# Reordering the head of an eight-core attention and feed-forward kernel: statistics tile by tile, GpSimd's rows as add then multiply, and one key unit of pair 1 in each token group

## The reference, cut to what matters

```
x = x + attn_block(layernorm(x))           # per batch entry x is [2048, 1024]
    # q, k, v = x@Wq, x@Wk, x@Wv ; 16 heads of 64
    # x' + softmax(q k^T / 8) v @ Wp, where x' is the normalised x
x = x + tanh(layernorm(x) @ W1 @ W2 @ W3 + bias)
```

## Time and profile before

| | |
|---|---|
| time, median of 3 runs | 729.91 us (729.40 to 729.97) |
| profiled execution: time | 729.96 us |
| its span on the slowest core (core 6) | 728.2 us |
| spans of the eight cores | 725.1 to 728.2 us |
| PE busy | 681.6 us (94%) |
| ACT busy | 599.4 us (82%) |
| DVE busy | 264.4 us (36%) |
| POOL busy | 125.3 us (17%) |
| exponentials on ACT | 512, 528.3 us |

### The profile page before, as it was taken

The page is one execution under the profiler, slowest core; times in us unless marked ns, Lnnn a source line. Parts: engine busy times, 40 slices in busy tenths (PEclk is TensorE's granted clock), DMA queues, the critical chain, the costliest instruction groups (busy, mean ns, idle before and its releaser), DMA issues.

```text
span 728.2 us, 21958 instructions; the slowest of 8 cores (725.1 to 728.2 us)
## 1 busy us (share of the span) xinstructions
PE 681.6 (94%) x9112; PEld 432.3 (59%) x9112; DVE 264.4 (36%) x590; ACT 599.4 (82%) x600; POOL 125.3 (17%) x169
## 2 busy tenths in 40 slices
PE   1699999999999999999999999999999989999996
PEld 0465676667666765676667656665676555444443
DVE  4724322332223322322332233224322343556663
ACT  2566999999999999999999989999999899444443
POOL 5871000000000002000000000012010121366654
PEclk9999999999999999999999999999999999999999
DMA  8959700111010004610110000032024000334332
GB/s 229 283 72 166 135 9 3 16 16 16 4 16 2 2 3 69 107 17 2 17 22 12 16 2 3 2 88 88 2 41 80 1 3 2 109 124 155 134 116 116
DMA packets 13344, 41.87 MB, mean 57 GB/s; under 512 B 1600, under 2 KB 1728, under 8 KB 13248
## 3 DMA queue, kind: packets, MB, share of 16 engines
q0 software_dynamic: 5904, 15.21, 13.7%
q1 hardware_dynamic: 7056, 25.17, 10.4%
q10 hardware_dynamic: 288, 0.10, 0.1%
HBM read 46.76 MB, written 8.39 MB: 76 GB/s over the span
## 4 chain that ended last, share of the span: by engine, by line
PE 86%; DVE 4%; issue 3%; DMA 3%; ACT 3%; POOL 0%; DVEq 0%; SPq 0%; ACTq 0%; POOLq 0%
PE sc L370 18%; PE pv L398 16%; PE fl L217 14%; PE fl L256 8%; PE sc L521 5%; PE fl L343 4%; PE fl L326 4%; PE sc L464 4%; PE fl L464 3%; ACT P L382 2%; DMA aoT<-x 2%; PE fl L422 2%; PE sc L217 1%; DMA wv<-wqkv 1%; PE pv L521 1%
## 5 line engine op out<-in xcount | busy, mean ns | idle before, releaser
L382 ACT ACTIVATE P<-sc,cb 128x1024 bf16<-128x1024 f32 x512 | 528.3, 1114 | 36.4 <-PE sc L370 24.4
L398 PEld LDWEIGHTS pv<-v,P 128*128 128x128 bf16 x4096 | 157.7, 97 | 44.1 <-issue 17.2
L398 PE MATMUL pv<-v,P 128*128 128x65 bf16 x4096 | 173.5, 193 | 5.4 <-DVE ao L414 2.6
L370 PE MATMUL sc<-qT,kT 64*128 64x256 bf16 x2048 | 157.5, 272 | 1.8 <-ACT P L382 1.8
L370 PEld LDWEIGHTS sc<-qT,kT 64*128 64x128 bf16 x2048 | 78.5, 94 | 42.8 <-issue 25.2
L532 ACT ACTIVATE S<-S 128x512 f32<-128x512 f32 x32 | 20.1, 629 | 58.2 <-DVE S L528 58.2
L256 PE MATMUL fl<-wv,S 128*128 128x128 bf16 x960 | 63.6, 219 | 1.8 <-DVE aoT L429 0.4
L256 PEld LDWEIGHTS fl<-wv,S 128*128 128x128 bf16 x960 | 54.1, 98 | 12.4 <-issue 12.2
L217 PE MATMUL fl<-S,wq 128*128 128x512 bf16 x224 | 57.8, 380 | 0.5
L217 PE MATMUL fl<-S,wk 128*128 128x512 bf16 x208 | 53.5, 380 | 3.1 <-DVE ao L414 1.3
L268 DVE CAST v<-fl 128x512 bf16<-128x512 f32 x29 | 20.0, 691 | 78.8 <-PE fl L256 78.8
(11 more groups left out here) (128 smaller groups left out, 555.8 us busy)
## 6 DMA issues: line engine op xcount, KB each, us to landing
xs<-x SPq DMA_DIRECT2D x22, 512.0 KB, 6.0
out<-S SPq DMA_DIRECT2D x15, 512.0 KB, 2.9
aoT<-x SPq DMA_DIRECT2D x8, 512.0 KB, 12.7
wk<-wqkv POOLq DMA_DIRECT2D x8, 256.0 KB, 9.0
wq<-wqkv POOLq DMA_DIRECT2D x8, 256.0 KB, 4.9
wv<-wqkv POOLq DMA_DIRECT2D x8, 256.0 KB, 5.9
bufA<-w1t POOLq DMA_DIRECT2D x4, 512.0 KB, 14.3
bufB<-w POOLq DMA_DIRECT2D x4, 512.0 KB, 25.0
```

The costliest lines, as they stand in the source:

```text
L370: ins = TE.matmul(sc[s][:, 512 * h + QC * i:512 * h + QC * (i + 1)], kT[p % 2][64 * h:64 * (h + 1), 128 * m:128 * (m + 1)], qT[p % 2][64 * ...
L382: exp_in[t] = s_se.inc(SE.activation(P[t % NPB][:], sc[s][:], AF.Exp, bias=cb[p % 2][:], scale=0.125))
L398: ins = TE.matmul(bank[PV0][:, col:col + 65], P[t % NPB][:, off:off + 128], v[p % 2][:, VW * (2 * m + h):VW * (2 * m + h) + 65], start=(u ...
```

## The change

Only the head and the share-out of filler units change:

- Statistics, epsilon and power are done for each tile alone (`ln1_tile`). DVE writes the negated mean (`ngm`), and GpSimd normalises as (x + ngm)·rs, so that its rows need no nm. For the first tile of a group GpSimd multiplies ngm·rs for ACT. Tile 15 is normalised by DVE. nm for all tiles, which the tail needs, is made once by DVE after the head.
- wk of pair 0 is issued only when tile 0 of x has landed, wq behind the row of tile 1 and wv behind that of tile 3, as before, and wk of pair 1 behind tile 5.
- PE's order in a group becomes: keys, queries, two turnings, values, two turnings, and then the keys of pair 1 of the same group. Before, all keys of pair 1 came later: groups 0 and 1 between the last units of the head, group 2 as the first filler of pair 0.
- At the end of the head the value unit of group 3 starts ahead of `guard1` and is cut 12 + 8 + 12 instead of 16 + 16.
- `N_FOLD` becomes [8, 4, 4, 4, 4, 4, 4], where it was [7, 4, 4, 4, 4, 5, 4]. The line for pair 3 is unchanged.

```diff
-        w_in = {(1, 0): load_slice(1, 0)}
+        w_in = {}
...
-        def ln1_stats(t):
+        def ln1_tile(t):
             need(VE, x_in[t])
             st = st6[t % 4]
             for h in range(2):
                 m = s_ve.inc(VE.bn_stats(st[:, 6 * h:6 * (h + 1)], x_tile[t][:, 512 * h:512 * (h + 1)]))
             need(VE, m)
-            return s_ve.inc(VE.bn_aggr(mv[:, 2 * t:2 * t + 2], st[:]))
...
+            m = s_ve.inc(VE.bn_aggr(mv[:, 2 * t:2 * t + 2], st[:]))
             need(VE, m)
+            s_ve.inc(VE.tensor_scalar(ngm[:, t:t + 1], mv[:, 2 * t:2 * t + 1], -1.0, None, ALU.mult))
+            m = s_ve.inc(VE.tensor_scalar(ve[:, t:t + 1], mv[:, 2 * t + 1:2 * t + 2], EPS, None, ALU.add))
             need(GP, m, gp_ones)
+            m = s_gp.inc(GP.tensor_tensor(rs[:, t:t + 1], ve[:, t:t + 1], mhalf[:, 0:1], ALU.pow))
+            if t % 4 == 0:
+                need(GP, m)
+                nm_in[t] = s_gp.inc(GP.tensor_tensor(nm[:, t:t + 1], ngm[:, t:t + 1], rs[:, t:t + 1], ALU.mult))
+                return
+            eng, sem = (VE, s_ve) if t == NT - 1 else (GP, s_gp)
+            need(eng, m, t1_mm.get(t - 2 * NXN))
+            xn_in[t] = sem.inc(eng.tensor_scalar(xn1[t % (2 * NXN)][:], x_tile[t], ngm[:, t:t + 1],
+                                                 rs[:, t:t + 1], ALU.add, ALU.mult))
...
+        need(GP, x_in[0])
+        w_in[(1, 0)] = load_slice(1, 0)
+        for t in range(4):
+            ln1_tile(t)
+            if t == 0:
+                ln1_se(0)
+            if t == 1:
                 w_in[(0, 0)] = load_slice(0, 0)
+            ln1_turn(t, SE, s_se)
+        w_in[(2, 0)] = load_slice(2, 0)
+        for g in range(NT // 4 - 1):
+            t0 = 4 * g + 4
+            for t in range(t0, t0 + 2):
+                ln1_tile(t)
+            ln1_se(t0)
+            if g == 0:
                 w_in[(1, 1)] = load_slice(1, 1)
+            bk = first_proj(1, 0, g)
+            bq = first_proj(0, 0, g)
+            evict_qk(1, 0, g, bk, SE, s_se)
+            for t in range(t0, t0 + 2):
+                ln1_turn(t, SE, s_se)
+                if t == t0:
+                    evict_qk(0, 0, g, bq, SE, s_se)
+            for t in range(t0 + 2, t0 + 4):
+                ln1_tile(t)
+            bv = first_proj(2, 0, g)
+            if t0 + 4 == NT:
+                for h in range(3):
+                    square(1, 0, h)
+                    square(0, 0, h)
+            ln1_turn(t0 + 2, SE, s_se)
+            evict_v(0, g, bv, SE, s_se)
+            ln1_turn(t0 + 3, *((VE, s_ve) if t0 + 4 == NT else (SE, s_se)))
+            bk = first_proj(1, 1, g)
+            evict_qk(1, 1, g, bk, SE, s_se)
...
-        run(unit_k(1, 1, squared=False))
+        b = next_bank()
+        values = v_mms(0, 3, b)
+        for _ in range(12):
+            next(values)
         guard1(0, next_bank())()
         for t in range(BATCH):
             emit_qk(t)
         guard2(0, next_bank())()
-        b = next_bank()
-        values = v_mms(0, 3, b)
-        for _ in range(16):
+        for _ in range(8):
             next(values)
         guard3(0, next_bank())()
...
-        N_FOLD = [7, 4, 4, 4, 4, 5, 4]
+        N_FOLD = [8, 4, 4, 4, 4, 4, 4]
...
-            for g in range(2 if p == 0 else 0, 4):
+            for g in range(3 if p == 0 else 0, 4):
                 units.append(unit_k(p + 1, g))
```

More of the change, by code:

```diff
@@ L89, in build_program @@
         biasb = sb("biasb", D, F32)
-        mhalf = sb("mhalf", 2, F32)
+        mhalf = sb("mhalf", 1, F32)
         st6 = [sb(f"st6_{i}", 12, F32) for i in range(4)]
@@ L96, in build_program @@
         nm = sb("nm", NT, F32)
+        ngm = sb("ngm", NT, F32)
         mv2 = sb("mv2", 2 * NT, F32)
@@ L560, in ln1_stats @@
             need(VE, m)
-            return s_ve.inc(VE.bn_aggr(mv[:, 2 * t:2 * t + 2], st[:]))
-        def ln1_power(t, n, m):
-            var = mv[:, 2 * t:2 * (t + n)].rearrange("p (t c) -> p t c", c=2)[:, :, 1]
+            m = s_ve.inc(VE.bn_aggr(mv[:, 2 * t:2 * t + 2], st[:]))
             need(VE, m)
-            m = s_ve.inc(VE.tensor_scalar(ve[:, t:t + n], var, EPS, None, ALU.add))
+            s_ve.inc(VE.tensor_scalar(ngm[:, t:t + 1], mv[:, 2 * t:2 * t + 1], -1.0, None, ALU.mult))
+            m = s_ve.inc(VE.tensor_scalar(ve[:, t:t + 1], mv[:, 2 * t + 1:2 * t + 2], EPS, None, ALU.add))
             need(GP, m, gp_ones)
-            m = s_gp.inc(GP.tensor_tensor(rs[:, t:t + n], ve[:, t:t + n], mhalf[:, 0:n], ALU.pow))
-            need(GP, m)
-        nm_in = {}
[L574 to L580, removed]
+            m = s_gp.inc(GP.tensor_tensor(rs[:, t:t + 1], ve[:, t:t + 1], mhalf[:, 0:1], ALU.pow))
[7 more added lines that the diff above has]
+                                                 rs[:, t:t + 1], ALU.add, ALU.mult))
+        nm_in = {}
         def ln1_se(t):
@@ L585, in ln1_se @@
                                               bias=nm[:, t:t + 1], scale=rs[:, t:t + 1]))
[L587 to L598, removed]
         def ln1_turn(t, eng, sem):
@@ L611, in ln1_turn, with first_proj @@
             S_in[t // 4].append(bank_free[b])
-        def first_proj(n, g):
+        def first_proj(n, p, g):
             b = next_bank()
-            run(v_mms(0, g, b) if n == 2 else proj_mms(n, 0, g, b))
+            run(v_mms(p, g, b) if n == 2 else proj_mms(n, p, g, b))
             return b
[L619 to L623, removed]
-                w_in[(0, 0)] = load_slice(0, 0)
-            if j == 1:
-                w_in[(2, 0)] = load_slice(2, 0)
-            if j == 5:
-                w_in[(1, 1)] = load_slice(1, 1)
[L629 to L643, removed]
@@ L646, in build_program @@
-        run(unit_k(1, 0, squared=False))
-        b = first_proj(1, 3)
+        need(GP, x_in[0])
[5 more added lines that the diff above has]
+            if t == 1:
+                w_in[(0, 0)] = load_slice(0, 0)
+            ln1_turn(t, SE, s_se)
[6 more added lines that the diff above has]
+            if g == 0:
+                w_in[(1, 1)] = load_slice(1, 1)
+            bk = first_proj(1, 0, g)
[17 more added lines that the diff above has]
+            evict_qk(1, 1, g, bk, SE, s_se)
@@ L648, in build_program @@
+        b = first_proj(1, 0, 3)
         evict_qk(1, 0, 3, b, VE, s_ve)
-        for g in range(3):
-            square(1, 0, g)
-            square(0, 0, g)
         square(1, 0, 3)
-        b = first_proj(0, 3)
+        b = first_proj(0, 0, 3)
         evict_qk(0, 0, 3, b, SE, s_se)
@@ L669, in build_program @@
         evict_v(0, 3, b, VE, s_ve)
-        for g in range(2):
+        for g in range(3):
             square(1, 1, g)
@@ L677, in build_program @@
         bias_in = d_b.inc(GP.dma_start(biasb[:], bias_d.partition_broadcast(128)))
-        need(VE, xn_in[NT - 2], xn_in[NT - 1])
+        need(VE, xn_in[NT - 4], xn_in[NT - 2])
+        s_ve.inc(VE.tensor_mul(nm[:], ngm[:], rs[:]))
         rs1_in = s_ve.inc(VE.tensor_scalar(rs1[:], rs[:], 1.0, None, ALU.add))
```

## The result

The changed kernel takes 738.21 us (median; 737.6 to 738.77) against 729.94 us of the kernel before: ratio 1.0114, 95% interval 1.0096 to 1.0131, so it is slower by 8.3 us. The forecast was 737.4 us, with a range of 732.5 to 740. A median here is over all executions of a kernel, some of which are slowed on one die by a lower clock, while a ratio compares only undisturbed executions with those of the kernel before measured beside them, so small differences between kernels are to be read from the ratios.

A forecast was written before the change was run, and what follows sets the result against it. PE was taken to bound the pairs, a chain of waits the head. Head -2.1, pair 5 -2.7, stall on W3 +11.3 and clock +1.0 gave +7.5 on 729.91 us: 737.4 us, range 732.5 to 740.

The forecast's parts named there:

- The step that decides: Pair 3's second slot: the first `unit_w123` moves there and waits for W3's four pieces; +11.7 us, 11.3 taken.
- Clock: Behind the stall on W3: PE may resume at a slower rate, costing 0 to 1.7 us; 1.0 taken.
- Pair 5: Pair 5 falls from 17 to 16 units: -2.7 us, at least the unit's own 1.73 us of PE.
- Head: Head: keys of group 0 start sooner, partly lost to waiting for pair 1's wk; -2.1 us, from -1.0 to -3.8.
- The 0.4 us that were to be given back: End of head: the value unit, with 12 matmuls behind `guard3` and its bank needed by third iteration's scores, loses 0.4 us.
- Rival 2: Pair 3: W3, its load the only traffic, arrives in time and nothing stands; -4.8 us, 725.1 us; chance 0.06.

The follow-up runs named there:

- the two shifts: Changed kernel with pair 3's early fold unit one slot or two slots later: 733.24 us (ratio 1.0057) and 729.15 us (ratio 1.0001).
- both edits: Changed kernel without pair 3's early line, with bank 7 for the head's last value unit and x tiles 8 to 15 held until wv landed: 729.17 us.

## Why the prediction was right

- *The step that decides* held as put: the last `unit_w12` in the last slot of pair 2, the first `unit_w123` in the second slot of pair 3, four waits for bufA. The landings after the first issue at 270.36 were 6.6, 10.7, 14.5 and 17.3 us, against 7.4, 11.8, 15.0 and 19.2 in the forecast's reckoning; the unit ended at 288.8; undisturbed it would run 2.5 us from the end of the products ahead of it, 275.7 to 278.2, so the stall is +10.5 us where 11.7 was worked out and 11.3 taken. Some 0.4 us of it is the last two matmuls at the lower clock, 1.01 us instead of 0.59. The old-head kernel with the new shares and the removal of the early line show the cause from both sides, and the two shifts show its size.
- *Clock.* 1.0 us was taken between 0 and 1.7. The interval of core 0 is 81.8 - 69.4 = 12.4 us longer than its own from pair 1 to 2, so 1.9 are left for the slower clock behind the unit: just over the upper bound, since the clock came back only 5 us after the unit's end. Together the two terms were taken as 12.3 us and measured 12.4, one 0.8 too large and the other 0.9 too small. The rule of the Trainium skill's page "TensorE: Matmul & The Clock Gate" (HAM oscillation), that a wait for data puts the array back to half its clock, holds in this trace on all eight cores, at 274.3 to 280.2 us. It does not hold for every wait: one slot later four cores waited up to 2.1 us for W3 and kept 1.00. The forecast took its 1.7 us from two units at what the page prints as the same clock. That print is no reading: the trace's record of the clock begins at 27.4 us (24.2 in the changed kernel), and the first keys' matmuls of 512 columns, ahead of it, take 586 to 631 ns, those behind it 376 to 379. The 1.7 us are the price of the half clock.
- *Pair 5* gave 2.6 us of the 2.7.
- *Head.* Keys of group 0 at 20.0 (forecast 19.9), values at 26.6 (26.6), wk of pair 1 landed at 30.5 (31.2) with a wait of 1.2 us on core 0 and 0.9 to 1.9 on the cores (1.9), `guard1` at 55.5 (55.8). The first exponential came 3.1 us sooner, 3.7 on the median core. The 0.4 us that were to be given back behind it were not: from there to pair 0's reduction the seven other cores take 58.1 to 59.2 us, where all took 58.5 to 59.5. Core 0 takes 60.7, some 2.5 us more, since its clock fell to 0.50 for 6.8 us from 58.3: a hazard the forecast did not have, met on one core in eight.
- *Luck in the number.* The head was forecast at -2.1 us. At pair 0's reduction the median core is 4.5 us ahead of the median core before, but core 0 only 1.4 ahead of core 6 before, because of that fall. Cores 2 and 6 have as long a stall (82.3 us) and no fall in the head, and their spans are 734.2 and 734.0 us, where core 0 has 736.3. Without the fall this execution would have taken an estimated 2.1 us less, 735.8, and the forecast would have been 1.6 too high, still in its range. A head gain taken too small and a hazard left out cancelled each other. In the same way the 11.3 us by which pair 3's interval grew agree with the term taken for the stall alone only because core 6 before had 70.5 us there, with a hole of 1.28 us at 290.1, where the median core had 69.1.
- *Rivals.* The rule of the Trainium skill's page "DMA: Bandwidth & Descriptors" ("Anatomy of one DMA") would have had all of W3 there in an estimated 6.8 us; the last piece landed 17.3 us after the first issue. The rows of the same load in the trace of before did price it. Rival 2's premise that this load is the only traffic was wrong: wk, wq and wv of the next pair are issued right behind it, from 272.4 us on, and land at 288.9 to 291.4. They stood behind it before as well, so its times to landing held; what W3 would take alone no run shows.
- *Missed term.* Without the stall the change should give 4.8 us, and the kernel without the early unit gave 2.2 to 2.7. On the cores' medians the head and the way to pair 1 give 3.5 and pair 5 2.6; but pair 3, with all its fold units at its end, takes 70.0 instead of 69.1 us, and the last stretch from pair 6's reduction to the end 189.2 instead of 187.9. That leaves 3.7 us on the median core and 2.9 on the slowest of the profiled executions. In pair 3 of the kernel without the early unit five of the eight cores have one hole of 0.5 to 1.3 us on PE, between 277 and 287 us, while W3 is loading or just behind it; its cause is open. Of the last stretch 1.0 us is the last store of `out`, whose code is unchanged. It lands 2.0 us after its issue in the kernel before and 3.0 in the changed one (core 0 before, then core 2 after, each from this store's issue to the end):

```profile
out<-S SPq DMA_DIRECT2D x1, 256.0 KB, 2.0
```

```profile
q14 instruction: 1, 0.01, 0.6%
...
out<-S SPq DMA_DIRECT2D x1, 256.0 KB, 3.0
```

  On all eight cores of the nine kernels in which this store takes 2.8 to 3.1 us, one 8 KB packet of the instruction queue starts 1.5 to 1.7 us after its issue, while it is under way. In the three others (the kernel before, the new shares with the old head, the key units outside the groups) it takes 2.0 to 2.2 us, and that packet starts 3.8 us or more after the issue, or within 0.4 us of it and ahead of the store's own packets. So the loss goes with where the fetch of the program happens to fall. No run varied that alone, so it is argued and not shown.

## What to carry to other kernels

Filler units that look alike need not be alike: moving one unit up a queue moves what it triggers, and what waits for that. After changing a share-out, find for each load the instruction that frees its buffer and the first one that reads it, and hold the distance against the load's own time to landing. A line that places a unit by its number in a queue (here the first of pair 3) must be looked at again when the number of another unit changes.

Where PE waits for ACT in a fixed rhythm, independent matmuls in the hole are worth more than the hole, since they can also keep the clock up: here some 2.8 us for the holes and 1.2 to 2.4 for the clock.

## What the runs showed of the hardware

- The granted clock fell after holes of quite different make: 4.2 us with two matmuls in them, but also where PE waited 2.2 us once or twice in the head and 4.07 us once. At like waits some cores fell and others didn't (four of eight one slot later, seven of eight with the key units outside the groups). A core that fell stayed at 0.50 for 3.4 to 13.7 us.
- A third level exists besides these two. In the kernel with the other value bank, core 4 (first line before, then in it):

```profile
600.00:629.00 29.00, 26.39 (x272) 14.96 (x276) 12.79 (x27) 18.56 (x21) 9.35 (x11) 1.00 0.18 59
630.00:634.50 4.50, 4.50 (x25) 2.17 (x24) 2.38 (x6) 2.67 (x3) 2.85 (x4) 0.81 0.09 36
```

  It comes at 630 us in four cores of one die at once, for 4.1 to 4.5 us, and at 660 us once more in two of them. In three other kernels (x held back, both edits, key units outside) it comes in two cores of one die at a time, from 631 us on, for 3.5 to 4.7 us. It is not in the profiled executions of the kernel before or after.
- A weight load issued by GpSimd beside x took 8.9 to 9.6 us to land on core 0 of the changed kernel (8.1 to 10.6 over its cores), whatever its place in the order. With x held back wk of pair 1 took 3.9 to 5.4 us. On core 0 of the changed kernel wk, wq, wv and the second wk landed at 17.4, 22.0, 26.5 and 30.5 us, one each 4.0 to 4.6 us.
- The trace's record of TensorE's clock begins only 21.7 to 28.8 us into the span in the kernels before and after, and views print 1.00 ahead of it, though matmuls there take 585 to 634 ns instead of 376 to 379.
